# A slot-pipelined convolution, top-k and token-attention kernel: small stages moved to other slots, VectorE's statistics and values put ahead of the second minimum

## What is computed

```python
xn = group_norm(x)                                  # a group is one channel of one image
y = conv7x7(xn, dilation 5, padding 15)             # 32 channels to 1
imp = sigmoid(gelu(batch_norm(y)))                  # (32, 110, 110)
idx = sort(top_k(imp, 192))                         # 192 pixels of each image
tokens = take(xn * imp, idx) + pos[idx]             # (32, 192, 32)
o = softmax(q @ k.T / 2) @ v                        # q, k, v = tokens @ w_qkv.T; 8 heads of 4
t1 = layer_norm(tokens + o @ w_o.T + b_o)
t2 = layer_norm(t1 + relu(t1 @ w1.T + b1) @ w2.T + b2)
out = x + put(xn * imp, idx, t2)                    # chosen pixels are replaced
```

## Time and profile before

| | |
|---|---|
| median of the runs shown | 1411.7 us |
| the profiled execution | 1413.15 us |
| its span, first to last instruction | 1411.3 us |
| TensorE, matmul busy | 1040.7 us (74%) |
| VectorE busy | 930.4 us (66%) |
| ScalarE busy | 709.7 us (50%) |
| GpSimd busy | 679.1 us (48%) |
| mean granted TensorE clock | 0.876 of full speed |

### The profile page before, as it was taken

How to read it: one execution, slowest core, us unless ns; L and a number is a source line. 1 busy time by engine, 2 the same in 40 slices (tenths; PEclk the granted TensorE clock), 3 DMA queues, 4 the chain that set the end, 5 groups by cost and what they waited for, 6 DMA issues and landing times. The chain is left out here.

```text
span 1411.3 us, 24956 instructions
## 1 busy us (share of the span) xinstructions
PE 1040.7 (74%) x7976; PEld 824.9 (58%) x7976; DVE 930.4 (66%) x2691; ACT 709.7 (50%) x1658; POOL 679.1 (48%) x949
## 2 busy tenths in 40 slices
PE   1496757679877897789778968797667668678646
PEld 1364545467756775577566756675546456566524
DVE  7244788677756876687668776777576775544524
ACT  1254333355635664566465745564445455557424
POOL 1132225614553674547653765376526645752354
PEclk9698888999978999799998998899879788889865
DMA  9498777655644887688758895666334535626559
GB/s 192 138 275 235 209 203 186 169 130 145 169 115 127 217 236 200 173 216 231 209 143 213 234 247 156 167 182 179 95 107 123 140 96 133 166 59 200 161 149 278
DMA packets 181238, 247.09 MB, mean 175 GB/s; under 512 B 70741, under 2 KB 77141, under 8 KB 181109
## 3 DMA queue, kind: packets, MB, share of 16 engines
q1 hardware_dynamic: 170613, 238.46, 62.2%
q10 hardware_dynamic: 2304, 4.65, 1.5%
q0 software_dynamic: 8192, 2.40, 1.2%
HBM read 123.61 MB, written 121.80 MB: 174 GB/s over the span
## 5 line engine op out<-in xcount | busy, mean ns | idle before, releaser
L1014 POOL TENSOR_SCALAR res<-res,mom 128x440 f32<-128x440 f32 (+1 forms) x256 | 155.3, 608 | 395.8 <-DVE res L1296 394.0
L867 ACT ACTIVATE pr<-sc,least 96x192 f32<-96x192 f32 x512 | 185.7, 413 | 317.4 <-DVE least L1259 316.9
L531 PE MATMUL cv<-X,w_conv 128*128 128x330 f32 (+1 forms) x1024 | 307.8, 426 | 13.2 <-POOL X L970 6.1
L649 PE MATMUL sc<-k_b,qm 128*96 128x192 f32 x1024 | 241.1, 363 | 42.6 <-issue 24.0
L1259 DVE TENSOR_REDUCE least<-sc 96x2 f32<-96x384 f32 x256 | 140.3, 550 | 171.4 <-PE sc L649 170.9
L838 ACT ACTIVATE wgt<-ib,eps_col,mom 128x440 f32<-128x440 f32 (+1 forms) x256 | 175.3, 691 | 103.0 <-PE ib L578 96.9
L531 PEld LDWEIGHTS cv<-X,w_conv 128*128 128x128 f32 x1024 | 192.4, 204 | 52.4 <-ACT cvr L824 18.0
L649 PEld LDWEIGHTS sc<-k_b,qm 128*96 128x96 f32 x1024 | 172.5, 184 | 60.3 <-issue 42.0
L810 ACT COPY xt<-xb 110x512 f32<-110x512 f32 x225 | 132.2, 588 | 136.6 <-PE xb L515 104.1
L515 PE MATMUL xb<-cst,X 128*110 128x128 f32 x900 | 153.0, 297 | 57.2 <-ACT xt L810 36.5
L662 PE MATMUL pp<-cst,pr 96*96 96x96 f32 x1024 | 140.0, 262 | 67.4 <-ACT pt L878 64.8
(11 more groups left out here) (174 smaller groups left out, 1468.6 us busy)
## 6 DMA issues: line engine op xcount, KB each, us to landing
table<-xt SPq DMA_DIRECT2D x240, 224.0 KB
rt<-table SPq DMA_DIRECT2D x240, 224.0 KB, 4.3
out<-res SPq DMA_DIRECT2D x320, 137.5 KB
X<-in_x SPq DMA_DIRECT2D x58, 412.5 KB, 5.8
X<-in_x SPq DMA_DIRECT2D x58, 343.8 KB, 5.1
conv_rows<-cvr SPq DMA_DIRECT2D x64, 188.0 KB
y<-conv_rows SPq DMA_DIRECT2D x64, 165.4 KB
out<-res SPq DMA_DIRECT2D x64, 68.8 KB
```

What stands on the lines that cost most here:

```text
L531: last = mm(cv[:, 0:CUT[half]], w_conv[:, 4 * q + z], X[:, m % XI, at0:at0 + CUT[half]], start=z == 0, stop=z == 3)
L649: last = mm(sc[0:HALF, k % 2, K * h:K * h + K], qm[:, 2 * pair + h, HALF * half:HALF * half + HALF], k_b[:, b, :], start=True, stop=True)
L867: last = A(pr[:, unit % 2, 2 * pair + h, :], sc[0:HALF, k % 2, K * h:K * h + K], ACT.Exp, scale=-1.0, bias=least[:, k % 2, h:h + 1])
L1014: last = gp.tensor_scalar(v, v, 1.0, mom[:, NB * g + b, 0:1], ALU.mult, ALU.add)
```

## The change

The table of slots is rewritten and some stages are cut in two. In group 0's numbers: the masks stay in slot 65, the running sums get slots 66 (greater) and 67 (equal), the ranks move from 66 to 68 and 69, the hot rows from 67 to 70 and 71, `pick` from 68 to 72, and the index from 69 to 72 and 73. The gathers start in slot 74 instead of 70 and run at three per slot (two in the last three slots) for nine slots instead of two per slot for twelve. `EMBED` on VectorE moves from 85 to 84, `project` from 87 to 86, the scores from 88 to 87, and the third set of scores starts ten slots after the first instead of twelve, so that the scores leave free slots 102 and 103, in which the next group's `pick` and index stand. `norm_first` moves from slot 116 to 115; GpSimd makes four masked copies of q in slot 86 ahead of `norm_last` and two each in slots 87 and 88. The first two tap sums move two and three slots later. The scatter and the way back keep their slots.

In VectorE's list the second minimum of a slot and `refine` now stand behind the statistics and the values. The masks of four images are two instructions instead of eight, and the index sums one comparison and one reduction per half instead of four accumulating comparisons.

```diff
-        TAPS, SUM, GELU, IMP_OUT, FLAT = (10, 17, 25, 31), (13, 20, 28, 33), 34, 36, 38
-        SEARCH, IMP_IN, MASKS, RANKS, PICK, INDEX = 40, 58, 65, 66, 68, 69
-        GATHER, REST, SPLIT, PARTS_OUT = 70, 74, (80, 84, 86), 90
-        EMBED, SCORES = 84, 88
-        MIX, SCATTER, BACK = SCORES + 27, SCORES + 34, SCORES + 40
+        TAPS, SUM, GELU, IMP_OUT, FLAT = (10, 17, 25, 31), (15, 23, 28, 33), 34, 36, 38
+        SEARCH, IMP_IN = 40, 58
+        MASKS, SCANS, RANKS, HOT, PICK, INDEX = 65, 66, 68, 70, 72, 72
+        GATHER, GATHERS = 74, (3, 3, 3, 3, 3, 3, 2, 2, 2)
+        REST, SPLIT, PARTS_OUT = 75, (83, 84, 85), 88
+        EMBED, PROJECT, SCORES = 82, 86, 87
+        MIX, NORM, FEED, NORM2 = SCORES + 27, SCORES + 28, SCORES + 30, SCORES + 33
+        SCATTER, BACK = SCORES + 35, SCORES + 41
...
-        for v, at0 in enumerate((0, 5, 12, 17)):
+        for v, at0 in enumerate((0, 5, 10, 17)):
...
-                    sc_read[p].append((idx_ok, upto(idx_ok, g)))
+                    sc_read[p].append((pick_rd, upto(pick_rd, g)))
...
-                for g, n in at(s, EMBED + 3):
-                    for j in range(4):
-                        masked(g, j)
-                for g, n in at(s, GATHER, 12):
-                    gather(g, 2 * n)
-                    gather(g, 2 * n + 1)
+                for k, first in enumerate((PROJECT, PROJECT, PROJECT + 1, PROJECT + 2)):
+                    for g, n in at(s, first):
+                        masked(g, k)
...
-                for b in range(NB):
-                    post(v.tensor_scalar(gt[:, b], imp[:, b], tb[:, b:b + 1], None, ALU.is_gt))
-                    post(v.tensor_scalar(eq[:, b], imp[:, b], tb[:, b:b + 1], None, ALU.is_equal))
+                level = tb[:].unsqueeze(2).to_broadcast([H, NB, H])
+                post(v.tensor_tensor(gt[:], imp[:], level, ALU.is_gt))
+                post(v.tensor_tensor(eq, imp[:], level, ALU.is_equal))
...
+                for g, n in at(s, GELU + 2):
+                    importance(g, 1)
                 for g, n in at(s, SCORES, U):
-                    for k in score_at.get(n, [])[0:2]:
+                    for k in score_at.get(n, [])[0:1]:
                         least_of(g, k)
...
+                for g, n in at(s, SCORES, U):
+                    for k in score_at.get(n, [])[1:2]:
+                        least_of(g, k)
+                for g, n in at(s, SEARCH, TOPK_STEPS):
+                    refine(g, n)
```

More of the change, by code:

```diff
@@ L760, in _ @@
                     offsets(g)
-                for g, n in at(s, MIX + 1):
+                for g, n in at(s, PICK):
+                    pick(g)
+                for g, n in at(s, NORM):
                     mix_out(g)
-                for g, n in at(s, MIX + 3):
-                    feed(g)
-                for g, n in at(s, MIX + 4):
+                for g, n in at(s, FEED + 1):
                     feed_in(g)
-                for g, n in at(s, MIX + 5):
+                for g, n in at(s, FEED + 2):
                     feed_last(g)
@@ L770, in _ @@
                     moments_spread(g)
-                for g, n in at(s, EMBED + 2):
+                for g, n in at(s, EMBED + 3):
                     tokens_turn(g)
-                for g, n in at(s, EMBED + 3):
+                for g, n in at(s, PROJECT):
                     project(g)
@@ L785, in _ @@
                         (values_turn if value_at[n][1] else values)(g, value_at[n][0])
-                for g, n in at(s, PICK):
-                    pick(g)
                 for g, n in at(s, MIX):
                     mix(g)
+                for g, n in at(s, FEED):
+                    feed(g)
         @block.scalar
@@ L1045, in _ @@
                     gp.tensor_tensor(rb[:], rb[:], tok_x[:, g % 2], ALU.add).then_inc(t2_ok, 1)
-                for g, n in at(s, EMBED + 3):
-                    for j in range(4):
-                        masked(g, j)
-                for g, n in at(s, GATHER, 12):
-                    gather(g, 2 * n)
-                    gather(g, 2 * n + 1)
+                for g, n in at(s, GATHER, len(GATHERS)):
+                    for k in range(sum(GATHERS[:n]), sum(GATHERS[:n + 1])):
+                        gather(g, k)
                 for g, n in at(s, SCATTER, 4):
@@ L1135, in find_masks, with find_equal @@
                     post(v.tensor_tensor_scan(cg[:, b], gt[:, b], zrow[:], 0.0, ALU.add, ALU.add))
+            def find_equal(g):
+                sync()
+                for b in range(NB):
                     post(v.tensor_tensor_scan(ce[:, b], eq[:, b], zrow[:], 0.0, ALU.add, ALU.add))
@@ L1156, in find_ranks, with find_hot @@
                 post(v.tensor_copy(startend[:, NB:2 * NB], cs[:, :, H - 1]))
-            def find_hot(g):
+            def find_hot(g, half):
                 sync()
-                for b in range(NB):
+                if half == 0 and g:
+                    dve.wait_ge(pick_ok, upto(pick_ok, g - 1))
+                two = range(2 * half, 2 * half + 2)
+                for b in two:
                     post(v.tensor_scalar(hot_a[:, b], iota_k, startend[:, b:b + 1], None, ALU.is_ge))
                 sync()
-                for b in range(NB - 1):
-                    post(v.scalar_tensor_tensor(hot[:, b], iota_k, startend[:, NB + b:NB + b + 1], hot_a[:, b],
-                                                op0=ALU.is_lt, op1=ALU.mult))
-                v.scalar_tensor_tensor(hot[:, NB - 1], iota_k, startend[:, 2 * NB - 1:2 * NB], hot_a[:, NB - 1],
-                                       op0=ALU.is_lt, op1=ALU.mult).then_inc(hot_ok, 1)
+                for b in two:
+                    ins = v.scalar_tensor_tensor(hot[:, b], iota_k, startend[:, NB + b:NB + b + 1], hot_a[:, b],
+                                                 op0=ALU.is_lt, op1=ALU.mult)
+                    if b < NB - 1:
+                        post(ins)
+                    else:
+                        ins.then_inc(hot_ok, 1)
             def find_rest(g):
@@ L1180, in find_index @@
                 dve.wait_ge(pick_ok, upto(pick_ok, g))
+                ranks = sc[0:HALF, half, 0:448].rearrange("p (b j) -> p b j", j=112)
+                below = junk[0:HALF].rearrange("p (b j) -> p b j", j=H)
                 sync()
[L1182 to L1185 removed]
+                link(v.tensor_scalar(below, ranks[:, :, 0:H], slot_col[:, half:half + 1], None, ALU.is_le))
+                post(v.reduce_sum(col[:, NB * half:NB * half + NB], below, AX))
+                sync()
                 if half == 0:
                     return
[L1188 removed]
                 for half in range(2):
                     ks = slice(NB * half, NB * half + NB)
[L1192 to L1195 removed]
+                    ranks = sc[0:HALF, half, 0:448].rearrange("p (b j) -> p b j", j=112)
+                    post(v.scalar_tensor_tensor(pixf[:, 2, ks], ranks[:, :, 110], float(H), col[:, ks], op0=ALU.mult, op1=ALU.add))
+                    last = v.scalar_tensor_tensor(pixf[:, 0, ks], col[:, ks], 480.0, ranks[:, :, 111], op0=ALU.mult, op1=ALU.add)
+                    if half == 0:
+                        post(last)
+                last.then_inc(pick_rd, 1)
+                dve.wait_ge(pick_rd, upto(pick_rd, g))
                 sync()
```

58 lines of the change are left out of this document (27 added, 31 removed).

## The result

| | before | after |
|---|---|---|
| median of the runs, us | 1414.2 (4 runs, 1411.1 to 1420.5) | 1380.8 (4 runs, 1378.7 to 1382.4) |
| span of the profiled execution, us | 1411.3 | 1380.6 |
| mean granted TensorE clock | 0.876 | 0.895 |

The ratio of the times is 0.9744, with a 95% interval of 0.9714 to 0.9774. The medians lie 33.5 us apart, 2.4%; by the ratio the change saves 2.6%, 36 us. The forecast was 43 us, so the kernel came out 12 us above the 1369 predicted, and inside the forecast's own range of 1350 to 1390.

What follows compares the result with a forecast made beforehand. No engine was full (TensorE busy 74%, VectorE 66%); most was to be won in the middle's long slots. Terms 14 + 31 + 8 - 20 + 10 = 43 us off 1413.15 gave 1370, 1369 against the median; range 1350 to 1390.

Steps and rivals of the forecast that it cites:

- Masks to index: Phases 5 to 13: cutting VectorE's long block saves 2 us in each of seven groups, 14 us; ends 0 and 6.
- not under 6: Phase 7, the slot with VectorE's long block, was to take under 6 us, with phases 8 to 12 near 5.
- The low end, 0: Masks to index: no gain per group if VectorE is the bound through all of phases 5 to 13.
- the block I had named: Phase 7: VectorE's 7.87 us without pause at importance, masks and running sums, with the next slot's `res` behind it.
- Projection: Phases 25 to 29: masked copies of q ahead of `norm_last` end the first scores' wait and slow clock, 31 us saved.
- Filling: Early slots: tap sums 4, refinement 7, masks to ranks 1, half lost at gathers, 2 more behind slot 84: 8 us saved.
- The sums' move: Filling: later tap sums shorten waits for their trip through memory, 2 us for each of two sums, 4 us.
- Gathers: Later, denser gathers, phases 14 to 24: GpSimd just fits, tokens come late; 20 us charged as a loss.
- Rival 3: GpSimd is the bound from first gather to tokens; six groups lose 4.5 us more each: 1396 us, chance 0.13.
- VectorE's order: Slots with two scores: statistics fill the second minimum's wait, net 2 us per group over five, 10 us saved.
- Moving the scores by a slot changes no work: Scores placed in other slots, way back keeping its slots: priced at nothing.

Runs made afterwards that it cites:

- the block back: Kernel after with both importance halves, masks and all running sums together again in one VectorE slot, ranks left in place: ratio 0.9718 to the kernel before.

## Why the prediction was right, and where it was off

The side and the range held, and no main term came out with the other sign: the total was 33.5 us of 43. It held partly by luck, because errors cancelled: three gains were put too high, and a gain about as large as any of them was put at nothing.

- **Masks to index, 14 forecast.** The pause of TensorE and the slow clock of the earlier trace rows did go: 0.94 after, in slot 187. But phase 7 is 7.4 us, not under 6, and phases 5 to 15 together went from 58.5 to 57.8. With the block back the slow clock is back as well and the time is not longer, so the slow clock was not what this stage cost. The low end, 0, was right for the block I had named; what little there may be comes from ranks and marks. The new forms of the masks and of the index instructions were not undone by any run. The Trainium skill (VectorE: DVE Perf Modes, "Mode 2×_2P — use both read ports for one tensor") does not let a `tensor_tensor` read one tensor through both ports, which spoke against the two wide mask instructions; they take 0.62 us each where nothing disturbs them, 1.2 together as estimated, and no run here compares the two forms element by element.
- **Projection, 31 forecast, 19 measured by undoing it.** The mechanism was right: wait gone, first scores at full speed. The new wait is 2.16 us in the rows shown and 11.2 in six groups (18.2 less the 7.0 that was there), 1.9 each and not 1.3. What I left out is that this pause has a slow stretch behind it, 0.71 in 821.3 to 826.6. I counted what a removed pause gives back in clock and not what a new pause takes; how much of the missing 12 us that is, no run separates.
- **Filling, 8 forecast.** Slots up to 89 gave 1.6 us. Up to slot 74 the kernel after is 7.9 us faster (208.3 to 200.4), and slots 75 to 89 take 6.3 of it back, 5.9 in slot 84 (8.0 to 13.9). Slot 84 takes 12.5 us with the order alone too, where the gathers stand as before, and 7.9 with the gathers late alone, so the late gathers by themselves do not make it long; why it is long stays open. The sums' move was priced by their waits while filling. It is worth 14.6 us in this schedule, by its place ahead of the index, a term that I did not have; against the kernel before it is a loss avoided.
- **Gathers, 20 charged, 22 measured alone.** The total agrees by luck. Alone, the tokens wait 18.6 us; in the kernel after they wait 41.0, where I had 20. I took the landing from group 7's end, and there the DMA engines had next to nothing to do. In the middle it takes 4.2 to 6.2 us, and groups 2 to 5 wait 1.7 to 5.7 and not 1.5. Groups 6 and 7 wait 7.1 and 14.3 us and not 5 and 6; their landings take only 3.5 and 3.7 us, so there the fault is another: in group 7 VectorE is at the tokens 22.7 us after the first gather, and 24 gathers take 33.3 to the issue of the last. Rival 3 was half true: GpSimd has no idle time between first and last gather but that of issuing, 38.8 us for 24 in group 4 (52.7 before).
- **VectorE's order, 10 forecast, 10 alone and some 20 undone.** Alone, it came out in size and place: 10.7 us in the middle. Phases 16 to 24 went from 35.7 to 32.2 us; 33.9 with the order alone and 33.7 with it undone say that about half of this is the order. The other half was not tried alone. Why undoing costs more, and most of it in the filling, stays open.
- **"Moving the scores by a slot changes no work": priced at nothing.** This is the step that failed. Phases 0 to 3 went from 23.7 to 18.5 us, mostly slot 183; over the four middle groups that is 19 us. They are 18 to 19 in every kernel built on the one after, whichever other part was undone (19.0 with the order back, 18.3 with the copies back), and 22.9 and 23.3 in the two built on the one before. So it comes from what those share, the new table of scores, mixing and feed-forward slots. That it is the filled pause of slot 182 is read from the trace and was not tried alone.

## What to carry to other kernels

Price a step that moves between slots by who stands next to it in its new slot, for every group whose phase it shares: one of the largest gains here (by the trace, scores into a slot where TensorE had a pause) and an unforeseen saving (a 1.57 us sum kept away from the index) were both in moves that change no work. Cutting a long block of one engine can be worth nothing: compare sums over all phases, not the block. Before a slow clock is priced, see which engine ends the stretch: beside VectorE's block, 5.2 us at 0.50 cost nothing. When a wait goes, look for the one that comes in its place: with the order alone 75 us went and 68 came. And take a transfer's landing from a stretch as loaded as the one that it will stand in.

## What the runs showed of the hardware

The landing of the last 96-row gather takes longer where the DMA engines are busier. Busy time and DMA share from its issue to the tokens, in the kernel after for groups 4 and 2, and in the kernel before for group 7 (the last column but one is the DMA share):

```profile
798.70:803.90 5.20, 2.33 (x18) 1.89 (x16) 0.54 (x4) 2.73 (x8) 4.92 (x7) 1.00 0.90 209
...
513.40:519.60 6.20, 2.26 (x17) 1.81 (x15) 0.45 (x4) 2.65 (x8) 5.88 (x8) 1.00 0.92 206
```

```profile
1219.00:1221.20 2.20, 1.95 (x12) 1.14 (x13) 1.17 (x5) 1.10 (x3) 2.15 (x4) 1.00 0.04 6
```

It took 5.2 and 6.2 us at shares of 0.90 and 0.92, and 2.2 at 0.04; group 7 of the kernel after lies between, 3.7 us at 0.71, and with the gathers a slot earlier it took 2.3 at 0.41. These are stretches found in the traces; no run changed the load alone. The Trainium skill (DMA: Bandwidth & Descriptors, "Latency and other measured facts") has memory answer some 2 us later under high load; the trace agrees in kind and shows more, 3 to 4 us.

The wide mask instruction has two lengths. VectorE's `gt` of one group, and GpSimd's row beside it:

```profile
716.55 1.26 POOL L974 TENSOR_SCALAR X<-X,mom 128x1100 f32<-128x1100 f32 x1
```

```profile
716.96 1.31 DVE L1135 TENSOR_TENSOR gt<-imp,tb 110x440 bf16<-110x440 f32 x1
```

Of its eight instances the four that start while L974 runs take 1.31 to 1.38 us, the other four 0.62. The Trainium skill (SBUF — State Buffer, "Who interferes with whom") says that a VectorE instruction with two inputs from SBUF contends with a GpSimd instruction that reads SBUF; the trace agrees. Here it costs 0.7 us in four groups. In group 4 VectorE works without a pause from this instruction to 727.76 us, so it may lie on the path; with the block in one slot again the instruction takes 0.62 us in all eight groups, and that kernel is not slower, but no run tried this alone.
